# Held accumulators, spread unit additions, 186 dense steps and 80-column windows in a graph-network kernel

## The reference

```python
dst = minimum((12500 * uniform(200000) ** 2.0).astype(int32), 99999)   # then sorted
...
agg = segment_sum(table[src], dst, num_segments=n)   # table: x, or x scaled per node
```

## Time and profile before

| | |
|---|---|
| median of 3 runs | 7995.45 us (7989.22 to 7995.82) |
| profiled execution, own time | 7993.52 us |
| its span in the trace | 7991.9 us |
| TensorE busy (matmul) | 5060.7 us, 63% |
| VectorE busy | 3914.0 us, 49% |
| ScalarE busy | 1935.0 us, 24% |
| GpSimd busy | 5477.0 us, 69% |

### The profile page before, as it was taken

One profiled execution on the slowest core, in us unless ns is written; L12 is line 12 of the kernel. 1 busy time (PEld: TensorE's weight loads), 2 busy tenths in 40 slices (PEclk: granted clock), 3 DMA queues, 4 the chain that ended last, 5 costly groups with the idle time before them and its releaser, 6 DMA issues. The chain is left out here.

```text
span 7991.9 us, 132850 instructions
## 1 busy us (share of the span) xinstructions
PE 5060.7 (63%) x32092; PEld 3580.7 (45%) x32093; DVE 3914.0 (49%) x17800; ACT 1935.0 (24%) x5420; POOL 5477.0 (69%) x4519
## 2 busy tenths in 40 slices
PE   0666666666666764277588549504775874775885
PEld 0555555555555553144344448402443443443444
DVE  4766666677777775622332563235224235223224
ACT  1333333344444553311011003202110102000103
POOL 0788888888888886377577571466775774775773
PEclk5888888888889887699799659757997996997998
DMA  7566666666666776666354117414443444443542
GB/s 213 61 65 65 68 69 74 75 83 85 87 94 95 101 105 125 221 186 190 117 182 156 48 43 200 131 45 158 151 152 106 158 142 132 151 150 100 166 158 80
DMA packets 945186, 957.03 MB, mean 120 GB/s; under 512 B 252756, under 2 KB 829883, under 8 KB 944722
## 3 DMA queue, kind: packets, MB, share of 16 engines
q0 software_dynamic: 316896, 288.98, 25.8%
q1 hardware_dynamic: 282692, 491.24, 19.1%
q10 hardware_dynamic: 345134, 171.70, 7.7%
HBM read 606.42 MB, written 327.65 MB: 117 GB/s over the span
## 5 line engine op out<-in xcount | busy, mean ns | idle before, releaser
L727 POOL DMA_INDIRECT work<-table,src_t x2385 | 2431.5, 1019 | 945.7 <-issue 713.7
L760 POOL DMA_INDIRECT sums<-work,idx x1564 | 2465.9, 1577 | 689.6 <-issue 384.8
L1256 PE MATMUL pp<-shared 128*128 128x378 bf16 (+8 forms) x8820 | 1928.0, 373 | 512.6 <-DMA shared<-counts 206.9
L1256 PEld LDWEIGHTS pp<-shared 128*128 128x128 bf16 x8820 | 899.5, 102 | 1352.0 <-issue 554.9
L1240 PE MATMUL pp<-work 128*128 128x128 f32 x4770 | 741.5, 304 | 744.6 <-DMA work<-table,src_t 544.8
L1678 DVE TENSOR_TENSOR acc<-acc,pp 128x128 f32 x597 | 172.3, 289 | 2012.7 <-PE pp L1240 2011.3
L1240 PEld LDWEIGHTS pp<-work 128*128 128x128 f32 x4770 | 657.8, 209 | 932.2 <-DMA work<-table,src_t 701.3
L1156 PE MATMUL pp<-acc 128*128 128x130 f32 x3128 | 554.8, 332 | 448.4 <-ACT work L913 448.4
L984 ACT ACTIVATE shared<-shared 128x128 bf16<-128x128 f32 x588 | 180.5, 307 | 2429.2 <-DVE shared L1685 1603.2
L1156 PEld LDWEIGHTS pp<-acc 128*128 128x128 f32 x3128 | 483.3, 235 | 470.7 <-issue 470.7
L913 ACT ACTIVATE work<-pp 128x520 f32<-128x520 f32 x391 | 236.2, 604 | 1328.8 <-DMA sums<-work,idx 1326.8
(11 more groups left out here) (307 smaller groups left out, 7022.8 us busy)
## 6 DMA issues: line engine op xcount, KB each, us to landing
shared<-counts SPq DMA_DIRECT2D x84, 661.5 KB
work<-table,src_t POOLq DMA_INDIRECT x2385
shared<-counts SPq DMA_DIRECT2D x42, 882.0 KB
shared<-counts SPq DMA_DIRECT2D x42, 840.0 KB
shared<-counts SPq DMA_DIRECT2D x42, 798.0 KB
shared<-counts SPq DMA_DIRECT2D x42, 787.5 KB
shared<-counts SPq DMA_DIRECT2D x42, 756.0 KB
shared<-counts SPq DMA_DIRECT2D x42, 735.0 KB
```

Of the source, the lines that this page charges most:

```text
L727: pool.indirect_dma_start(out=msg[:, i % SLOTS, k, :], out_offset=None, in_=table, in_offset=bass.IndirectOffsetOnAxis(ap=src_t[:, at:at + ...
L760: pool.indirect_dma_start(out=sums0[k], out_offset=bass.IndirectOffsetOnAxis(ap=picked, axis=0), in_=rows, in_offset=None, bounds_check=NP ...
L1256: i = pe.matmul(bank[c][:, 0:COLS[n]].rearrange("p (k w) -> p k w", w=PACK * w), x3[:, b % 2, h, part3, :], ring[:, q % RING, 0:TB * COLS[ ...
```

## The change

It has four parts, for each of layers 1 to 3.

1. ScalarE copies each of the five banks of pass 0 to SBUF (`held`, `hold(c)`) as soon as it is complete, between its tile parts. The first product of pass 1 in a bank waits for this copy, not for VectorE's additions. The units of pass 0 are added from the copy.
2. The units of pass 0 are added 6 in a step, those of pass 1 24 in a step as before. By the loop's numbers the 252 units of pass 0 fall in steps 88 to 129, and those of pass 1 come as 24, 6, 24, 24, 24, 24, 6 in steps 181 to 187.
3. The 2940 products are spread over 186 steps (15 or 16 in a step) and not 196; the tile parts follow at the same rate.
4. The window of a step has 80 columns and not 128: the 0/1 matrices, the products and the additions. The numbers that feed the flag and its loop are set to match. VectorE reads the first nodes of six steps at once.

```diff
+DENSE_STEPS = SPARSE - 13
+HELD_A_STEP, LAST_A_STEP = 6, 24
+HOLD_TILE = NT + 2
+SW = 80
...
-        hot = part(work, 4656, (3, KC, WIN))
+        hot, hot_x = part(work, 3072, (3, KC, SW)), part(work, 3072, (KC, WIN))
+        held_at = 3072 + 3 * KC * SW
+        held = [part(work, held_at + sum(COLS[0:n]), (COLS[n],)) for n in range(BANKS)]
...
+        products_by = lambda step: min(step * PRODUCTS // DENSE_STEPS, PRODUCTS)
+        tiles_by = lambda step: TB + 1 + step * TILES // DENSE_STEPS
...
+                def hold(c):
+                    act.wait_ge(chunk_done, DONE0 + (layer - 1) * CHUNKS + chunk_of(0, NB - 1, c) + 1)
+                    act.activation(held[c], bank[c][:, 0:COLS[c]], ACT.Copy).then_inc(held_made, 1)
+
                 for n in range(TILES + 1):
+                    if 0 <= n - HOLD_TILE < BANKS:
+                        hold(n - HOLD_TILE)
                     if n < TILES:
                         top_part(n)
...
-                        if b % NB == 0:
-                            pe.wait_ge(unit_added, ADDED0 + (layer - 1) * NU + (SLOTS * T0[n - BANKS + 1] if n >= BANKS else 0))
+                        if b == 0:
+                            pe.wait_ge(unit_added, ADDED0 + (layer - 1) * NU)
+                        if b == NB:
+                            pe.wait_ge(held_made, HELD0 + (layer - 1) * BANKS + c + 1)
...
-                    for m in range(PER_STEP * step, min(PER_STEP * (step + 1), BLOCKS * PER_BLOCK)):
+                    for m in range(products_by(step), products_by(step + 1)):
                         products(m)
...
-                        j = dve.tensor_scalar(hot[:, i % 3, k, :], iota[:, :], rel_t[:, at:at + 1], None, ALU.is_equal)
+                        j = dve.tensor_scalar(hot[:, i % 3, k, :], iota[:, WIN - SW:WIN], rel_t[:, at:at + 1], None, ALU.is_equal)
...
+                        of = bank[c] if p else held[c]
...
-                        dve.tensor_tensor(acc[:, ds(base[u], w)], acc[:, ds(base[u], w)], bank[c][:, at:at + w], ALU.add)\
+                        dve.tensor_tensor(acc[:, ds(base[u], w)], acc[:, ds(base[u], w)], of[:, at:at + w], ALU.add)\
...
-                    base = dve.value_load(base_row[0:1, GD + i:GD + i + 1], min_val=0, max_val=N - 1)
+                    if i % SLOTS == 0:
+                        _, bases = nc.values_load_multi_w_load_instructions(
+                            base_row[0:1, GD + i:GD + min(i + SLOTS, SPARSE)], engines=[mybir.EngineType.DVE], min_val=0, max_val=N - 1,
...
-                    wanted = max(SLOTS * T0[n + 1] if asked[n] <= i + 1 else 0 for n in range(BANKS))
-                    todo = max(min(whole, done + UNITS_A_STEP), wanted)
+                    todo = min(whole, done + (HELD_A_STEP if done < SLOTS * T0[BANKS] else LAST_A_STEP))
```

More of the change, by code:

```diff
@@ L167, in program @@
         width_step = part(shared, at0 + 36, (2, len(SPANS)))
-        assert at0 + 36 + 2 * len(SPANS) <= 10752
+        at0 += 36 + 2 * len(SPANS)
+        g_reach, g_past = part(shared, at0, (NQ,), i32), part(shared, at0 + NQ, (NQ,), i32)
+        assert at0 + 2 * NQ <= 10752
         ubase_bc = part(shared, 0, (NU,), i32)
@@ L484, in program @@
         chunk_of = lambda p, b, c: (p * NB + b) * BANKS + c
-        last_step = lambda q: (q * TB * PARTS + TB * PARTS - 1) // PER_STEP
+        products_by = lambda step: min(step * PRODUCTS // DENSE_STEPS, PRODUCTS)
+        last_step = lambda q: min(i for i in range(DENSE_STEPS) if products_by(i + 1) >= (q + 1) * TB * PARTS)
+        tiles_by = lambda step: TB + 1 + step * TILES // DENSE_STEPS
         FILL = EROWS // (EP * TURNS)
@@ L534, in _ @@
                 near = min(max(GD - q * P, 0), m)
-                for of, a, z in ((g_far, 0, near), (g_extra, near, m)):
+                for of, a, z in ((g_far, 0, near), (g_past, near, m)):
                     if a < z:
@@ L1267, in sums @@
                     pe.wait_ge(hot_ready, (layer - 1) * SPARSE + step + 1)
-                    window(step % 3, step % SLOTS, step % 3, chunks_in(step)).then_inc(summed, 1)
+                    window(step % 3, step % SLOTS, hot[:, step % 3, :, :], chunks_in(step), SW).then_inc(summed, 1)
                 pe.wait_ge(added, layer * SPARSE)
@@ L1279, in sums @@
                                 pe.sem_clear(x_hot)
-                                window(0, 0, 0, KC).then_inc(x_sum, 1)
+                                window(0, 0, hot_x, KC, WIN).then_inc(x_sum, 1)
             sums(1)
@@ L1439, in _ @@
             for m, q in ((P, slice(0, NQ - 1)), (GREST, slice(NQ - 1, NQ))):
[L1440 removed]
+                dve.tensor_copy(g_span[0:m, q], g_max[0:m, q])
+                i = dve.tensor_scalar(g_reach[0:m, q], g_max[0:m, q], float(WIN - SW), None, ALU.add)
             i.then_inc(prep, 1)
@@ L1661, in _ @@
             dve.wait_ge(key_step, KEY0 + 5)
+            dve.tensor_scalar(rel_t[:, 2 * NU:NCOL], rel_t[:, 2 * NU:NCOL], float(WIN - SW), None, ALU.add)
             dve.tensor_scalar(rel_t[:, 0:2 * NU], rel_t[:, 0:2 * NU], -float(FAR), None, ALU.add).then_inc(key_step, 1)
@@ L1709, in add_units @@
                         w, p, c = WIDTH[n], n // BANKS, n % BANKS
+                        of = bank[c] if p else held[c]
                         if u == SLOTS * T0[n]:
-                            dve.wait_ge(chunk_done, DONE0 + (layer - 1) * CHUNKS + chunk_of(p, NB - 1, c) + 1)
+                            if p:
+                                dve.wait_ge(chunk_done, DONE0 + (layer - 1) * CHUNKS + chunk_of(p, NB - 1, c) + 1)
+                            else:
+                                dve.wait_ge(held_made, HELD0 + (layer - 1) * BANKS + c + 1)
                         if u == u0:
@@ L1727, in sums @@
                 make_hot(0)
-                done = 0
+                done, made = 0, TB
                 for i in range(SPARSE):
@@ L1731, in sums @@
                         make_hot(i + 1)
-                    tile_parts(TB + i)
-                    base = dve.value_load(base_row[0:1, GD + i:GD + i + 1], min_val=0, max_val=N - 1)
+                    for n in range(made, tiles_by(i)):
+                        tile_parts(n)
+                    made = tiles_by(i)
+                    if i % SLOTS == 0:
+                        _, bases = nc.values_load_multi_w_load_instructions(
+                            base_row[0:1, GD + i:GD + min(i + SLOTS, SPARSE)], engines=[mybir.EngineType.DVE], min_val=0, max_val=N - 1,
+                            skip_runtime_bounds_check_because="a group's base is one of its edges' destination nodes")
                     dve.wait_ge(summed, first_window + i + 1)
```

30 lines of the change are left out of this document (15 added, 15 removed).

## The result

The changed kernel takes 7695.7 us (median of 4 runs, 7693.9 to 7705.9) against 7995.6 (4 runs, 7989.2 to 7997.1): a ratio of 0.9629, interval 0.9612 to 0.9646. Forecast were 7748, with 7700 to 7805 as the range for 8 in 10: the direction and the two large terms were right in kind, the size was 52 us short and 4 us beyond the range's end. The profiled execution took 7693.9 us, its span is 7692.3.

A forecast was written before the change was run, and what follows sets the result against it. It took the pace of GpSimd's gathers to bound layers 1 to 3. 7993.5 - 194.1 - 103.0 + 39 + 9 + 2 = 7746, and 7748 as the median lies 2 us higher; range for 8 in 10: 7700 to 7805.

The forecast's parts named there:

- the last window is added 7.6 us after the last gather: Step for each layer's end: with TensorE and VectorE caught up, the last window's addition follows by 7.6 us, not 42.
- the lead: Slack of 20 us: a gather waits for the window six steps back, 31.8 us later, which is there after 11.4.
- The waits of the middle (-194): Mid-layer, gathers' waits for TensorE's windows while VectorE adds pass 0's units vanish: -194.1 us, 64.7 a layer.
- The end of the layer (-103): Units of pass 1 end in step 187, so the last window comes sooner after the last gather: -103.0 us.
- The new wait in the second burst (+39): Steps 181 to 187: adding pass 1's units now makes gathers wait, 13 us a layer, +39; bounds 0 to 102.
- Additions from SBUF (+9): Pass 0's 252 additions a layer, both operands in SBUF, slow the gathers by 3 us a layer, +9.
- The third rival: Rival, chance 0.06: each addition from SBUF holds the gathers for its whole 0.167 us, 126 us, giving 7865.
- The rate and the 80 columns (0): More products in TensorE's step and narrower windows both lie beside the gathers, so they change the time by 0.
- Once (+2): Ten small VectorE instructions that run once, one of 796 columns: +2 us, bounds 0 to 4.
- no second wait: Rival, chance 0.15: the burst of pass 1's units makes no gather wait, so 39 us less, 7709.
- Waits moved: Rival, chance 0.14: waits move rather than go; no lead remains at the second burst, 34 us a layer, 7811.
- TensorE the bound: Rival, chance 0.02: TensorE, not the gathers, bounds the kernel; no total time given.

The follow-up runs named there:

- e2: Changed kernel, but the units of pass 0 added 24 in a step from their copy, not 6; 8462.3 us, ratio 0.9856 to the kernel before, slower chip.
- c1: The changed kernel as it is, run again on a slower chip; 8248.7 us, ratio 0.9654 to the kernel before.
- c2: The kernel before, unchanged, run again on a slower chip for its profile; 8545.0 us, a single launch.
- e1: Changed kernel with windows of 128 columns again, one held bank moved in SBUF; 8307.5 us, ratio 0.9674 to the kernel before, slower chip.
- e6: Changed kernel with one more VectorE comparison over 256 columns, SBUF to SBUF, in each step; 8265.7 us, ratio 0.9674 to the kernel before, slower chip.
- e4: Changed kernel with the 252 additions of pass 0 left out in each layer; 8277.6 us, ratio 0.9637 to the kernel before, slower chip.

## Why the prediction was right or wrong

The two large terms have the right mechanism; the misses are small ones, all to the same side. Two steps failed: "the last window is added 7.6 us after the last gather" (4.3 us measured), on which the end of the layer and the lead rest, and the term for what VectorE does to the gathers, +9 for the additions from SBUF and nothing for the rest, where the additions cost 0 and the rest fell by 13 us.

**The waits of the middle (-194): right.** They are gone to the last one, and e2 puts them back, at 58 us a layer on its chip, with TensorE free of the additions. The reckoning by which VectorE's lateness alone makes them (its additions, less its room, less the gathers' lead) gave 63 for the kernel before, where 64.7 was measured.

**The end of the layer (-103): right in kind, 10 us short.** The failed step here is "the last window is added 7.6 us after the last gather". I took 7.6 us from a single pair of rows and took it for the time that rows need to land. What stood there was TensorE's queue. This is TensorE of the kernel before around that window:

```profile
4420.67 4.26 PE L1256 MATMUL pp<-shared 128*128 128x450 bf16 x15
```

Its 15 products, with a granted clock of 0.71 in that stretch, lie ahead of the window of group 191, whose products start at 4424.8; at 1.00, 15 products of nearly that width take 2.93 us. Over steps 5 to 84 of that layer the time from the fourth gather's start to the window's addition has a median of 5.7 us, from 3.8 to 10.0. At the layer's end the changed kernel has no products left, and TensorE starts the last window 2.5 us after the last gather began:

```profile
4387.78 2.00 PE L1256 MATMUL pp<-work 128*128 128x80 f32 x8 [3.31 <-DMA work<-table,src_t]
4391.65 1.57 PE L1256 MATMUL pp<-work 128*128 128x80 f32 x6 [1.87 <-DMA work<-table,src_t]
```

**The new wait in the second burst (+39): there, where it was put, but 24 and not 39 us.** Partly the same error: the first window of the table is added 8.8 us after its gathers began and not 11.6, so the lead was 2.8 us longer than I took it. The burst's own steps make the rest: from there to the last window of the table they take 64.6 us and not 66.4 (steps of 12.1 us and 3.6 against the 12.3 and 4.2 that I used). 13 less 2.8 less 1.8 is 8.4, and 7.6 to 8.1 is measured. (The sum for the time after which a window is there gives 11.3 and not 11.4; the lead stays 20.) By my table two groups would wait, 5 and 7 us; the first of them just didn't. On the chip of c1, where the lead is nearly used up, three did.

**Additions from SBUF (+9): they cost nothing, and the pace came out 13 us better for another reason.** It is the largest miss, 22 us. The gathers' mean can't settle it: the same kernel's differs by 8 ns between two executions, which is 6 us a layer. What settles it is to sort the gathers of a trace by what VectorE ran beside them. This is a long gather of the kernel before, with the two instructions of a tile's parts:

```profile
3584.02 0.35 DVE L1685 SCALAR_TENSOR_TENSOR shared<-X,w_t,shared 128x128 f32<-128x128 f32 x1
3584.08 1.37 POOL L727 DMA_INDIRECT work<-table,src_t  x1 [0.30 <-issue]
3584.28 0.29 DVE L1694 TENSOR_TENSOR shared<-shared 128x128 bf16<-128x128 f32 x1
```

And these are the two gathers of the changed kernel that ran beside the six held additions shown above (3903.35):

```profile
3903.03 1.01 POOL L737 DMA_INDIRECT work<-table,src_t  x1 [0.30 <-issue]
3904.35 1.01 POOL L737 DMA_INDIRECT work<-table,src_t  x1 [0.31 <-issue]
```

Counted over all three layers, 544 of the 2385 gathers of the kernel before have the subtraction of line 1694 beside them, and take 1062 ns on average; the other 1841 take 1007. In the changed kernel 543 have it (line 1715 there) and take 1037, the other 1842 again 1007. That is 30.3 us against 16.0, which is all of the gain in pace and a little more. The held additions have no part in it: 240 gathers had one or more beside them and not the subtraction, with a mean of 1007.1 and none over 1019, against 1007.3 for the 1602 that had neither. So the term is 0.

The split is the same in all twelve traces (1006 to 1010 ns without the subtraction, 1024 to 1062 with it). It depends on where the subtraction falls: in the kernel before a gather takes 1089 ns if it begins in the gather's first 0.5 us, and 1021 if in the next 0.5. Whether the subtraction does it or the instruction of line 1685 just ahead of it can't be told apart, and why it costs less after the change isn't shown. On the three slower chips it makes 9 to 14 us in the seven runs with 80 columns and 17 to 21 in the three with more work for VectorE (c2, e1, e6). So the width may act by moving the subtraction; that is one execution each, and not a proof.

The third rival, a gather held for the whole of each held addition, is refuted by the same count, and by e4, where 126 us would have shown. The rule of the Trainium skill behind it ("SBUF — State Buffer", "Who interferes with whom") says that a VectorE instruction with two SBUF inputs contends with a GpSimd instruction that reads SBUF. The trace agrees with it for the tile parts, which are of that kind (1062 against 1007 ns), and not for the held additions, which are too (1007.1).

**The rate and the 80 columns (0): not refuted.** The columns alone gave 0.9999 where TensorE nearly sets the pace; on the first chip they weren't tried alone, and part of the 13 us above may be theirs or the rate's.

**Once (+2), against -3.3 elsewhere.** 5 us. Of it 2.5 lie before the first gather of layer 1 (3333.7 against 3336.2); in the other runs that gather starts between 3332.4 and 3340.2 with either kernel, so this is within the spread.

Together: 15 + 10 + 22 + 5 = 52 us, all of one sign. Only the new wait was inside its own bounds. The pace was outside them (-13 against 0 to 30), and so was the last term (-3 against 0 to 4); the end had been given none. The bound for VectorE's effect on the gathers, 16 us a layer, was drawn from the mean and the shortest gather; from the median it is 12, and by the count above 10. The range was drawn about the likeliest values with little room towards "no second wait", whose case alone was put at 7709, and none for several small terms going the same way.

**The rivals.** No second wait: refuted, 8 us a layer. Waits moved: refuted on the first chip. TensorE the bound: refuted there, from 3440 to 3540 us it is granted 0.93 of its clock, as before. On the other chips it is close to the bound with either kernel, and the change gains nearly the same. The 5.28 us of this rival's sum are of a stretch granted 0.60, so not all of them were at the lower level. The stretch on the first chip:

```profile
3440.00:3540.00 100.00, 78.86 (x435) 46.94 (x436) 25.28 (x126) 12.13 (x38) 76.83 (x77) 0.93 0.67 196
```

## What to carry to other kernels

When one engine issues at a fixed pace and others must only keep up on average, ask of each burst behind it three numbers: its extra work, the room in the steps that it covers, and the lead that the buffers give. Work beyond the sum came back here as waiting; the same work spread below the room cost nothing. What must be freed first, here a PSUM bank by a copy, may gain little by itself and still be what makes the spreading possible. Read a latency that several terms rest on from many pairs of rows, and look at what stood in the queue ahead of the one that you take. Before an interference is priced from a mean, sort the instructions by what ran beside them: here the whole excess lay in a quarter of them, beside one line.

## What was not expected of the hardware

The same two kernels ran 7% slower on other chips (8545 against 7996 us, 8249 against 7696), with the gain between them nearly the same in microseconds. None of it lies in layer 0 (the first gather of the kernel before starts at 3337.7 and at 3336.2 us); 396 of its 550 us lie in the three stretches of gathers (1250.4, 1245.6 and 1248.2 us, first to last), and 50 in the ends of the layers. There stand GpSimd's "remote" waits of about 2.1 us each, and stretches in which TensorE's products come 0.7 or 1.4 us apart with the engine waiting for nothing that the profile shows: 1.2 us in each steady step of the first layer in c2. Its granted clock from 3440 to 3540 us is 0.80 (c2) and 0.82 (c1), not 0.93. This is TensorE of the changed kernel there:

```profile
3701.94 0.34 PE L1274 MATMUL pp<-shared 128*128 128x432 bf16 x1 [0.39 <-issue]
3703.37 0.35 PE L1274 MATMUL pp<-shared 128*128 128x432 bf16 x1 [1.08 <-issue]
3704.07 0.52 PE L1274 MATMUL pp<-shared 128*128 128x432 bf16 x1 [0.36 <-issue]
```

What TensorE waits for in them, whether the lower clock is their cause or comes of them, and what "remote" is, stays open.
